# Scattering expert output rows by choice and token in a routed mixture-of-experts kernel, and reading them back as plain blocks

## The reference

```python
x = x + 0.5 * ffn(layernorm(x))       # called f1 below
x = x + attention(layernorm(x))       # la
x = x + 0.5 * ffn(layernorm(x))       # f2, same weights as f1
```

```python
mla_out = attention_16_heads(hs) @ o_w + o_b
probs = softmax(mla_out @ router_w + router_b)
topw, topi = top_k(probs, 2);  topw = topw / (topw.sum(-1) + 1e-8)
h1 = gelu(mla_out @ w1[e] + b1[e])            # for each expert e, 256 -> 512
h2 = h1 @ w2[e] + b2[e]                       # 512 -> 256
return hs + 0.3 * sum over the two chosen e of topw * h2[e]
```

## Time and profile before

| | |
|---|---|
| median of 3 runs | 2254.07 us |
| the profiled execution | 2247.4 us, span 2245.7 us |
| PE busy | 1848.4 us, 82% of the span |
| DVE busy | 1484.8 us, 66% |
| POOL busy | 553.3 us, 25% |
| experts f1m, first to last output tile | 650.8 to 841.2 us |
| attention la | 843.8 to 1336 us |
| experts f2m, first to last output tile | 1961.4 to 2152.1 us |
| combine | 2154.6 to 2245.7 us |

### The profile page before, as it was taken

How to read it: one execution, slowest core, us unless ns; L and a number is a source line. 1 busy time by engine, 2 the same in 40 slices (tenths; PEclk the granted TensorE clock), 3 DMA queues, 4 the chain that set the end, 5 groups by cost and what they waited for, 6 DMA issues and landing times. The chain is left out here.

```text
span 2245.7 us, 40893 instructions
## 1 busy us (share of the span) xinstructions
PE 1848.4 (82%) x12392; PEld 1021.6 (45%) x12393; DVE 1484.8 (66%) x3529; ACT 936.7 (42%) x1694; POOL 553.3 (25%) x640
## 2 busy tenths in 40 slices
PE   1799999999759994999999954899999998499930
PEld 1433333332249982676666641223333332299920
DVE  2678888888244444888887743878888884344423
ACT  0156666666612222444444310266666667122200
POOL 2222232331122214111110002213323311322256
PEclk9889999999979996999999975799999999699965
DMA  8325333321022223111110024354333220122245
GB/s 195 64 54 131 66 59 67 70 54 22 13 72 74 71 69 129 29 39 39 39 39 12 19 52 86 63 119 91 64 61 69 56 34 12 57 74 70 73 138 183
DMA packets 154622, 153.21 MB, mean 68 GB/s; under 512 B 20364, under 2 KB 145036, under 8 KB 154124
## 3 DMA queue, kind: packets, MB, share of 16 engines
q1 hardware_dynamic: 113600, 98.95, 19.5%
q10 hardware_dynamic: 30636, 27.21, 4.5%
q0 software_dynamic: 10240, 25.18, 4.0%
HBM read 86.60 MB, written 58.20 MB: 64 GB/s over the span
## 5 line engine op out<-in xcount | busy, mean ns | idle before, releaser
L588 DVE TENSOR_REDUCE f_M<-bank 128x1 f32<-128x512 f32 x1024 | 674.6, 686 | 193.4 <-PE bank L858 183.5
L498 ACT ACTIVATE f_PT<-bank 128x512 f32<-128x512 f32 x1024 | 572.9, 596 | 295.5 <-PE bank L875 290.7
L858 PE MATMUL bank<-f_KS,f_QS 96*128 96x512 bf16 x1024 | 404.1, 401 | 75.8 <-DVE f_M L588 39.9
L875 PE MATMUL bank<-f_QS,f_KS 99*128 99x512 bf16 x1024 | 394.0, 389 | 44.4 <-ACT f_PT L498 31.5
L875 PEld LDWEIGHTS bank<-f_QS,f_KS 99*128 99x128 bf16 x1024 | 99.7, 99 | 421.9 <-ACT f_PT L498 304.8
L885 PE MATMUL bank<-f_PT,f_V 128*32 128x512 f32 x2048 | 273.0, 607 | 0.0
L858 PEld LDWEIGHTS bank<-f_KS,f_QS 96*128 96x128 bf16 x1024 | 100.9, 99 | 206.1 <-DVE f_M L588 138.5
L1119 PE MATMUL bank<-f_room,f2m_gT 128*128 x568 | 136.0, 383 | 0.3 <-ACT f2m_gT L1055 0.3
L1119 PE MATMUL bank<-f_room,f1m_gT 128*128 x568 | 136.0, 383 | 0.1
L427 POOL DMA_INDIRECT routed_rows<-f_AO,f_rows_i x128 | 124.6, 973 | 42.1 <-issue 42.1
L1055 ACT ACTIVATE f1m_gT<-f1m_hb 128x512 f32<-128x512 f32 x71 | 44.7, 630 | 155.2 <-DVE f1m_hb L1076 155.2
(11 more groups left out here) (254 smaller groups left out, 2922.8 us busy)
## 6 DMA issues: line engine op xcount, KB each, us to landing
f_QS<-q_parts SPq DMA_DIRECT2D x192, 64.0 KB
f_KS<-k_parts SPq DMA_DIRECT2D x168, 64.0 KB
expert_rows<-f1m_y ACTq DMA_DIRECT2D x71, 128.0 KB, 1.8
expert_rows<-f2m_y ACTq DMA_DIRECT2D x71, 128.0 KB, 1.7
xr<-f_xr SPq DMA_DIRECT2D x16, 512.0 KB, 3.1
f_room<-in_L_ffn_w SPq DMA_DIRECT2D x2, 4096.0 KB, 21.6
q_parts<-f_q SPq DMA_DIRECT2D x16, 384.0 KB, 2.5
k_parts<-f_k SPq DMA_DIRECT2D x16, 384.0 KB, 2.5
```

Of the source, the lines that this page charges most:

```text
L498: act.activation(PT[:, i % 8, :], SCE[i % 2][:, :], ACT.Exp).then_inc(probs_ready, 1)
L588: dve.tensor_reduce(M[:, t, h:h + 1], SCM[(a * SC + i) % 3][:, :], AX.X, ALU.max).then_inc(scm_drained, 1)
L858: pe.matmul(SCM[(a * SC + i) % 3][:, :], QS[par][0:K_MAX, h, t * P:(t + 1) * P], KS[par][0:K_MAX, h, :], start=True, stop=True).then_inc(s ...
L875: pe.matmul(SCE[i % 2][:, :], KS[par][0:K_EXP, h, t * P:(t + 1) * P], QS[par][0:K_EXP, h, :], start=True, stop=True).then_inc(sce_filled, 1)
```

## The change

An expert's output row is no longer put where its tile lies but where its reader wants it: row `choice * 4096 + token` of `expert_rows`. For that each routed row gets a tail of two floats: the row it was sent to as first choice, and the token's number. A row of `routed_rows` is now 130 floats. An expert tile reads its rows with the tails. DVE compares the first tail value with the row's own place (`OWN`): if they are equal the row is a first choice, if not a second one, and 4096 is added to the token. The result, `dest`, is the index of one indirect DMA on POOL per tile (unused rows go to 128 rows behind the end). That scatter takes the place of ACT's plain store, and it waits for the scatter before it to have landed.

The readers use plain DMAs of 512 KB, two per batch. In `la` the first two are on SP, right behind the load of the first `xr`, the others on POOL. In `combine` all sixteen are on SP, without a wait between them, each into a buffer of its own; the output is stored by ACT. The residual for `combine` is loaded during the f2 experts, one batch at every fourth slot from slot 8. ROW, IDX and the five instructions that made IDX are gone. The slots of `experts` are all written out, without a loop.

```diff
@@ attend_and_route: the tail, the table
+LAT, RW = H * KPH, H * KPH + TAIL                     # 128, 130
-            own(dve.tensor_scalar(tiles[:, :], tiles[:, :], -float(P), float(REG), ALU.mult, ALU.add))
-            own(dve.tensor_tensor(unused..., ROW..., w["region"][:, 1:E]..., ALU.is_ge))
-            own(dve.tensor_tensor(unused..., unused..., tiles[:, 0:E - 1]..., ALU.mult))
-            own(dve.tensor_reduce(less[:, :], unused[:, :, :], AX.X, ALU.add))
-            own(dve.tensor_tensor(IDX..., ROW..., less[:, :], ALU.subtract))
+            own(dve.tensor_tensor(OWN[:, :], at[:, :], w["partition"][:, 0:1].to_broadcast([P, NT]), ALU.add))
...
-                s.own(dve.tensor_scalar(ROW[:, ds((a - START) * T, T), :], rows_f[:, :, :], 0.0, None, ALU.add))
+                dve.tensor_copy(AO[par][:, :, LAT], rows_f[:, :, 0])
+                dve.tensor_scalar(AO[par][:, :, LAT + 1], w["token"][:, :], float((a - START) * S), None, ALU.add)
                 dve.tensor_copy(rows_i[:, :, :], rows_f[:, :, :]).then_inc(rows_ready, 1)
@@ experts, SP
-                wait(sp, xT_filled, j + (BASE - 1))
+                    wait(sp, dest_ready, BASE + j - 1)
                     sp.dma_start(XN[:, buf, :], xs[ds(at, P), :]).then_inc(x_loaded[buf], 16)
+                load_late(sp, s)          # slot 1: b2; in f2 slots 8, 12, ... 36: one batch of xr
@@ experts, POOL
                     pool.tensor_copy(W1[:, buf, :], w["w1"][:, ds(e * F, F)]).then_inc(w1_ready, 1)
+                if tile(s, 2):
+                    j, buf = tile(s, 2)
+                    pool.wait_ge(y_ready, BASE + j + 1)
+                    if j:
+                        pool.wait_ge(y_stored[1 - buf], stored(j - 1))
+                    pool.tensor_tensor(pool_carrier[:, j:j + 1], zero[:, :], zero[:, :], ALU.add)
+                    pool.indirect_dma_start(
+                        out=ys, out_offset=bass.IndirectOffsetOnAxis(ap=dest[:, j:j + 1], axis=0),
+                        in_=Y[:, buf, :], in_offset=None).then_inc(y_stored[buf], 16)
@@ experts, ACT
-                    act.wait_ge(y_ready, j + (BASE + 1))
-                    act.dma_start(ys[ds(j * P, P), :], Y[:, buf, :]).then_inc(y_stored[buf], 16)
@@ experts, DVE, behind the copy of XT
+                    dve.tensor_scalar(offset[:, j:j + 1], XN[:, buf, LAT:LAT + 1], OWN[:, j:j + 1], float(B * S),
+                                      ALU.not_equal, ALU.mult).then_inc(offset_ready, 1)
+                    dve.wait_ge(offset_ready, BASE + j + 1)
+                    dve.tensor_tensor(dest[:, j:j + 1], offset[:, j:j + 1], XN[:, buf, LAT + 1:RW], ALU.add) \
+                       .then_inc(dest_ready, 1)
@@ combine
+            for b in range(B):
+                for n in range(2):
+                    at = n * B * S + b * S
+                    sp.dma_start(R[b][:, :, n, :], ys[at:at + S, :].rearrange("(t p) d -> p t d", p=P)).then_inc(rows_loaded[b], 16)
-                    for t in range(T):
-                        for n in range(2):
-                            pool.indirect_dma_start(
-                                out=R[i][:, t, n, :], out_offset=None, in_=ys,
-                                in_offset=bass.IndirectOffsetOnAxis(ap=idx[i][:, t, n:n + 1], axis=0),
-                            ).then_inc(gathered[i], 16)
@@ attention_pass
             load_x(0)
+            load_rows(sp, 0)
             load(sp, la_loaded)
...
-                pool.wait_ge(idx_ready, a + 1)
-                        pool.indirect_dma_start(out=R[:, t, n, :], ...)
+            for a in range(1, B):
+                pool.wait_ge(rows_read, a)
+                load_rows(pool, a)
```

More of the change, by code:

```diff
@@ L173, in attend_and_route @@
         rec = sb("rec", [P, T, H])
-        AO = [sb(f"AO{i}", [P, T, H * KPH]) for i in range(2)]
+        AO = [sb(f"AO{i}", [P, T, RW]) for i in range(2)]
         aoT = sb("aoT", [P, S])
@@ L1036, in _ @@
         def _(pool):
[L1037 to L1045 removed]
+            pool.memset(zero[:, :], 0.0).then_inc(zeroed, 1)
+            pool.wait_ge(zeroed, nth + 1)
@@ new lines, in _ @@
+            for s in SLOTS:
+                if tile(s, 0):
+                    j, buf = tile(s, 0)
+                    e = pool.value_load(tables[0:1, 0, j:j + 1], min_val=0, max_val=E - 1)
+                    wait(pool, h_filled, BASE + j - 1)
+                    pool.tensor_copy(W1[:, buf, :], w["w1"][:, ds(e * F, F)]).then_inc(w1_ready, 1)
+                if tile(s, 2):
[7 more added lines that the diff above has]
+                        in_=Y[:, buf, :], in_offset=None).then_inc(y_stored[buf], 16)
@@ L1216, in add @@
+            for b in range(B):
+                dve.wait_ge(rows_loaded[b], 32)
                 for n in range(2):
                     for t in range(T):
-                        last = dve.scalar_tensor_tensor(Y[i][:, t, :], R[i][:, t, n, :], cw[i][:, t, n:n + 1],
-                                                        Y[i][:, t, :] if n else XR[i][:, t, :], ALU.mult, ALU.add)
+                        last = dve.scalar_tensor_tensor(XR[b][:, t, :], R[b][:, t, n, :], CW[:, b * T + t, n:n + 1],
+                                                        XR[b][:, t, :], ALU.mult, ALU.add)
@@ L1220, in add @@
                     last.then_inc(half_ready if n == 0 else y_ready, 1)
                     if n == 0:
[L1222 to L1233 removed]
+                        dve.wait_ge(half_ready, b + 1)
@@ L1924, in attend_and_apply_experts, with load_late @@
                 w["b2"] = inner.enter_context(nc.sbuf_tensor(f"{tag}_b2", [P, E * D], F32))
-                experts(nc, sem, tag + "m", nth, xs, ys, bank, ident, w, w2_loaded, load_b2, routing, dims, NT)
+                last = nth == 1
+                XR = [inner.enter_context(nc.sbuf_tensor(f"{tag}_xr{b}", [P, S // P, D], F32)) for b in range(B)] if last else []
+                def load_late(sp, slot):
+                    if slot == 1:
+                        load_b2(sp)
+                    if last and slot >= 8 and slot % 4 == 0 and slot // 4 - 2 < B:
+                        b = slot // 4 - 2
+                        sp.dma_start(XR[b][:, :, :], xr[b].rearrange("(t p) d -> p t d", p=P)).then_inc(xr_loaded, 16)
+                experts(nc, sem, tag + "m", nth, xs, ys, bank, ident, w, w2_loaded, load_late, routing, dims, NT)
+                if last:
+                    combine(nc, sem, "fc", XR, xr_loaded, ys, out, routing, dims)
         load_and_make()
@@ L1946, in macaron @@
         attend_and_apply_experts("f2", 1, x2)
-        combine(nc, sem, "fc", 0, xr, ys, out, routing, dims)
 _INS = ["L0_attn_x", "L0_attn_Wq", "L0_attn_Wk", "L0_attn_Wv", "L0_attn_betas", "L0_attn_Wo",
```

310 lines of the change are left out of this document (109 added, 201 removed).

## The result

The changed kernel takes 2295.22 us (median of 4 runs, 2294.83 to 2297.36), the kernel before 2254.52 beside it (4 runs, 2248.26 to 2256.01): ratio 1.0188, 95% interval [1.0168, 1.0208], or 40.7 us. The forecast was 2278, the range 2228 to 2314. The two profiled executions differ by more than the medians, 49.9 us (spans 2245.7 and 2295.6): that of before took 2247.4 us, 7.1 less than its median, and that of the changed kernel 2297.36, 2.1 more.

A forecast was written before the change was run, and what follows sets the result against it. It took PE to bound the experts (2.72 us slot) and POOL's one-by-one gathers to end `combine`. Terms 72.8 + 5.1 + 5.1 - 12.1 - 49.3 + 3 = +24.6 us gave 2278 us, range 2228 to 2314.

The forecast's parts named there:

- The pace: Experts: 3.24 us per slot against 2.72, over 140 steps +72.8 us; bounds +22 and +113.
- The choice of 0.67: Experts, POOL: 0.67 us from carrier start to scatter start, taken from the `send_rows` scatter; bounds 0.33 and 0.76.
- The 0.20 for the size: Experts: landing of 128 KB takes 0.2 us more than the 2.37 seen for 64 KB; bounds 0 and 0.4.
- the loop written out: Experts: writing out all slots costs 0, nothing seen for or against.
- The residual's loads: f2 experts: eight 512 KB loads each delay a landing by up to 1.5 us; 0 to 12, taken as +3.
- Block ends: Ends of f1 and f2 experts: last scatter and POOL's long drain take 7.3 us for 2.16, +5.1 each.
- `la` and `combine`: `la`: first adds 6.1 us after block start, not 18.24, -12.1; `combine`: 41.8 us against 91.1, -49.3.
- the two rates: `combine`: DMA at 311 or 381 GB/s, middle 346 taken; gain -45.6 to -52.4 us.
- Warm scatters: Rival, experts: closely following scatters start after 0.33 us, pace 2.90, total 2231 us; chance 0.24.
- Size for nothing: Rival, experts: landing stays 2.37 us whatever the size, pace 3.05, total 2252 us, no change; chance 0.13.
- The second loop: Experts: through PE and POOL's weight copy behind the scatter, 6.10 us per two slots, 3.05 each; binds only if quicker.
- loop one: Experts, POOL: carrier, scatter, its landing, next carrier; 3.24 us per slot, bounds 2.70 and 3.53, sets the pace.

The follow-up runs named there:

- late_xr: Changed kernel with the residual loaded at the start of `combine` by ACT's queue, not during the f2 experts: 2299.9 us.
- split: Changed kernel with an added small POOL op that waits for the output tile, so the carrier waits only for the landing: 2249.8 us.
- land: Changed kernel in which, up to tile 63, a scatter no longer waits for the one before to land: 2209.5 us.
- merged_split: Changed kernel, landing awaited only from tile 64 (at a carrier with one wait), weight copy before the scatter, `combine` inside the f2 experts' block: 2195.2 us.
- w1first: Changed kernel with POOL's weight copy moved one slot ahead, in front of the scatter: 2313.3 us.

## Why the prediction was right, and where its sum was short

**The pace: right, and by the loop named.** The parts were 0.67 + 2.37 + 0.20 = 3.24; measured 0.65 + 2.59 = 3.24. The choice of 0.67 was right for a reason that the prediction didn't have: the row of `send_rows` has a carrier with several waits, as the new one. The 0.20 for the size is there too (2.59 - 2.37 = 0.22). By the rule of the Trainium skill, page "DMA: Bandwidth & Descriptors", section "Anatomy of one DMA — SWDGE (gpsimd) path", an estimate for 128 KB is 2.30 us. The trace shows 2.4 from issue to landing in the median, and 2.59 to the carrier that it wakes; the measurement decides.

**The mean slot: a little short, and the loop written out was put at nothing.** The usual slot is 3.22 to 3.24, the mean of f1m 3.30: 11 of its 70 slots take 3.5 to 4.1, 5.9 us more than usual in all. Some landings are late, in late_xr and split too, and the trace says what moves meanwhile. Two of the core's DMA queues, q8 and q14, carry instructions, in packets of 16 and 8 KB. Of 69 stretches from a scatter to the next carrier in f1m, 19 are 2.75 us or longer, and in every one of the 19 such a packet moves; of the 50 shorter ones 3 have one, none of q8. In f1m of split it is 15 of 15 and 8 of 54, in f2m of late_xr 15 of 15 and 5 of 55. In f1m of the changed kernel, with its slots written out, 12 and 17 packets move, in that of the kernel before, with its loop, 1 and 1. So it is most likely the code that the written-out slots bring with them that holds up these 19 landings, by 7.6 us in all. The sum had 0 for the written-out loop, "nothing seen for or against". That the packets come with the late landings is shown; that the loop would have saved these microseconds is not, since no kernel here has both loop and scatter.

**The residual's loads: the term that was mis-sized, +3 for +16.** The estimate was up to 1.5 us per load, with 12 as its top. late_xr gives 16.3. The landing behind such a load is about 2 us late, where 1.5 was the upper bound for one. What the sum didn't have at all is what follows: PE idles for 2 us at a stretch, and in four of the eight places its clock then falls. Of the 16.3 us 6.5 are that. The mechanism, a landing held up by the load, was the one named; its size and the clock were not. The general slot of the changed kernel leaves PE idle too, but in short pieces, and the clock stays at 1.00 there.

**Block ends: 5.1 for 7.6 and 8.3.** The steps left out a wait: the last scatter, too, waits for the one before. From the last output tile's start to its scatter it is 3.08 us (884.43 to 887.51), where the sum had 0.42 + 0.17 + 0.67 = 1.26. From there to the next block it is 7.10 (to 894.61), for 0.96 + 5.26 + 0.25 = 6.47. The guess that the long drain isn't the routing block's alone was right.

**`la` and `combine`: right within 1.6 and 2.5 us.** `la`'s first adds came 7.7 us after the block's start, not 6.1. `combine` ran at 370 to 385 GB/s in its middle, so nearer to the upper of the two rates.

**The rivals.** "Warm scatters" had a real number (0.34 from carrier to scatter) and a false cause: not what POOL did in between but how many semaphores the carrier waits for. Its pace was 0.33 + 2.37 + 0.20 = 2.90, and split, which has the 0.34, shows 2.86 in the usual slot. That split takes 2249.8 and not 2231 comes from the late landings and the residual's loads: its blocks are 214.0 and 223.5 us, where 70 steps of 2.90 are 203. "Size for nothing" is out by 2.59 against 2.37. The second loop, which that rival needs, was put at 3.05 with a carrier-to-scatter step of 0.67. Land shows it with 0.34, for which the prediction's own sum gives 2.88, and the slots are 2.79 in the mean: the sum is at most some 0.1 too long there. With two waits at the carrier no run shows the second loop by itself, and it didn't matter while loop one held.

**Where the gain of the readers went.** They save 62.3 us (10.5 and 51.8). The experts take back 97.8 and the block ends 15.9. Of the 97.8, the landing wait is nearly all: f1m and f2m without it (land) are 6.3 and 7.2 us over the kernel before.

**How near, and by what.** In the two profiles the sum is short by 25.3 us: 17.5 in f2m, 4.5 in f1m, 5.7 at the block ends and 1.6 in `la`, less 2.5 in `combine` and 1.5 elsewhere. The medians miss the forecast by 17 only, mostly because the profiled execution of before was a quick one; that part is luck. The sign isn't: every large term came with the sign and through the wait that the prediction named.

## What to carry over

A DMA that waits for its predecessor's landing turns a latency that nobody saw into a loop with a pace of its own: add up issue, landing and wake-up (here 3.24 us) and set them against the slot (2.72) before moving a store to such a queue; or order by landing only those DMAs that can meet in the same rows. In such a loop everything that delays a landing counts in full, large background loads first of all (16.3 us in f2m), while without the wait the same loads cost 1.2 us. Follow the idle time from the engine that waits to what its releaser itself stood behind: "PE waits for the weight copy" was true in every slot, and moving the copy made the kernel slower.

## What was not expected of the hardware

- On POOL, the gap between a small op and the indirect DMA behind it is 0.45 to 0.48 us where the op waits for two semaphores and the later in program order is met last (all of the changed kernel's f1m but the first tile), and 0.15 where it waits for one, whether a DMA (merged_split) or an engine (land) releases it. A second small op of 0.19 us that takes one of the waits saves 45 us over 140 tiles. Some gaps with two waits are longer: 0.57 at the first gather of `la`, whose carrier waits for `init` and `idx_ready`, and 0.75 to 0.77 four times in f2m of w1first.
- POOL's drain at a block's end is 0.4 to 0.7 us without indirect DMAs, 2.76 with one, 7.07 with 71.
- Where DMAs of 64 and 128 KB moved in the same 0.6 us the landing came 0.34 us later (w1first; read from the windows, not tried); behind 512 KB it came 2 us later.
- Packets of the instruction queues go with late landings: all 19 of 2.75 us or more in f1m, up to 3.45 where 2.58 is usual.
- Idle stretches of about 2 us in f2m, in which PE otherwise keeps the clock 1.00, were followed by 3 to 4 us at the lower level in four of eight cases (after 1.92, 2.05, 2.06 and 2.20 us, but not after 1.94, 1.96, 1.96 and 2.19); idle times of 0.23 us in every slot were not.
